# Layer two of a graph network on one core: one tile of picks in every sixteenth group becomes a gather, and the loops are four bodies long

## The reference

```python
src_feats = node_features[src]                                  # 200,000 rows of 64
messages = gelu(concatenate([src_feats, edge_features]) @ W_msg + b_msg)
agg = segment_sum(messages, tgt)
out = gelu(((1 + eps) * node_features + agg) @ W_upd + b_upd)
```

## Time and profile before

| | us |
|---|---|
| median of 3 runs | 2611.68 (2607.0 to 2617.65) |
| the profiled execution | 2620.69 |
| its span | 2618.9 |
| its loop of layer two with the last body, from the first gather to the last message sum | 1506.2 |

### The profile page before, as it was taken

The page is one execution under the profiler, slowest core; times in us unless marked ns, Lnnn a source line. Parts: engine busy times, 40 slices in busy tenths (PEclk is TensorE's granted clock), DMA queues, the critical chain, the costliest instruction groups (busy, mean ns, idle before and its releaser), DMA issues.

```text
span 2618.9 us, 70760 instructions
## 1 busy us (share of the span) xinstructions
PE 2437.3 (93%) x21749; PEld 2273.1 (87%) x21750; DVE 2012.4 (77%) x4216; ACT 1560.6 (60%) x5144; POOL 1791.4 (68%) x1879
## 2 busy tenths in 40 slices
PE   1588899999888888899999999999999999999998
PEld 1477799999888888899999999999999999999998
DVE  7888887766888886777777777777777777777774
ACT  2466666665666664566555656665656566556653
POOL 3377765677777773477777777777777777777771
PEclk9999999999999998899999999999999999999997
DMA  6111111111111110344444444445454544445451
GB/s 117 38 26 27 25 24 21 25 26 26 26 25 24 25 25 22 86 122 119 120 119 121 118 122 118 122 118 125 116 121 120 121 119 119 119 120 120 118 121 37
DMA packets 472280, 213.80 MB, mean 82 GB/s; under 512 B 264668, under 2 KB 441656, under 8 KB 472196
## 3 DMA queue, kind: packets, MB, share of 16 engines
q1 hardware_dynamic: 412548, 151.55, 22.1%
q0 software_dynamic: 59648, 61.20, 12.8%
HBM read 207.09 MB, written 5.51 MB: 81 GB/s over the span
## 4 chain that ended last, share of the span: by engine, by line
PE 58%; DVE 0%; ACT 0%; issue 0%; DVEq 0%
PE ps L930 43%; PE ps L1135 7%; PE ps L1000 4%; PE ps L1124 3%; PE ps L1082 1%; PE ps L1029 0%; DVE rows L1473 0%; DVE parts L1231 0%; DVE sel L1469 0%; DVE room L1675 0%; ACT h_sb L860 0%; DVE h_sb L1706 0%; DVE h_sb L1711 0%; ACT h_sb L878 0%; DVE tick L1510 0%
## 5 line engine op out<-in xcount | busy, mean ns | idle before, releaser
L639 POOL DMA_INDIRECT rows<-p_table,idx x1176 | 1109.8, 944 | 390.0 <-issue 342.8
L930 PE MATMUL ps<-parts,pick_all 128*128 128x448 f32 x5488 | 1162.0, 369 | 2.6 <-DVE parts L1231 2.6
L930 PEld LDWEIGHTS ps<-parts,pick_all 128*128 128x128 f32 x5488 | 1019.4, 189 | 77.7 <-issue 2.9
L639 POOL DMA_INDIRECT rows<-h_table,idx x688 | 665.3, 967 | 324.3 <-issue 200.9
L940 PE MATMUL ps<-hot_c,hot_p 128*128 128x150 f32 (+4 forms) x2336 | 435.0, 313 | 64.9 <-issue 37.1
L1469 DVE TENSOR_TENSOR sel<-ps,mask 128x896 f32<-128x896 f32 x196 | 214.0, 1092 | 307.0 <-PE ps L930 298.3
L940 PEld LDWEIGHTS ps<-hot_c,hot_p 128*128 128x128 f32 x2336 | 371.7, 192 | 85.7 <-issue 63.8
L731 ACT COPY adj<-ps 128x500 f32<-128x500 f32 (+4 forms) x880 | 349.9, 448 | 149.5 <-PE ps L940 136.9
L1452 DVE TENSOR_SCALAR pick_all<-src_all,node_f 128x1792 fp32r<-128x1792 int16 x196 | 406.5, 2074 | 27.4 <-issue 24.7
L1406 DVE TENSOR_SCALAR hot_p<-iota_p,scal 128x128 f32<-128x128 f32 (+2 forms) x880 | 301.1, 342 | 76.5 <-PE ps L940 56.0
L1473 DVE TENSOR_REDUCE rows<-sel 128x128 f32<-128x896 f32 x196 | 342.7, 1749 | 6.7
(11 more groups left out here) (182 smaller groups left out, 2345.0 us busy)
## 6 DMA issues: line engine op xcount, KB each, us to landing
src_all<-keys SPq DMA_DIRECT2D x196, 448.0 KB
ea<-in_edge_attr_dram SPq DMA_DIRECT2D x196, 256.0 KB
rows<-p_table,idx POOLq DMA_INDIRECT x1176
rows<-h_table,idx POOLq DMA_INDIRECT x688
x_sb<-in_x_dram SPq DMA_DIRECT2D x6, 224.0 KB, 4.3
h_table<-h_sb SPq DMA_DIRECT2D x6, 224.0 KB
p_table<-h_sb SPq DMA_DIRECT2D x6, 224.0 KB
out_dram<-h_sb SPq DMA_DIRECT2D x6, 224.0 KB
```

The lines of the kernel that those rows point to most:

```text
L639: nc.gpsimd.indirect_dma_start(out=rows[:, s, j, 0:D], out_offset=None, in_=table[:, :], in_offset=bass.IndirectOffsetOnAxis(ap=idx[:, s, ...
L930: last = nc.tensor.matmul(to, hot[:, k, t * P:(t + 1) * P], parts[:, part, k, :, :].rearrange("p a d -> p (a d)"), start=(k == 0 and part ...
```

## The change

In one group of sixteen (slot 3 of every fourth body) tile 6 is gathered by POOL, as tiles 0 to 5 are, and TensorE and VectorE pick tile 7 alone. That is 12 groups of 196; the last body has none. The pick matrix is still made for both tiles. The loops of POOL, TensorE and VectorE have four bodies in a pass and run 12 times; TensorE's and VectorE's announce their branch back. ScalarE's and SyncE's loops are as they were. VectorE's wait for slot 3 counts the additional gathers.

```diff
+    LOOP = 4
+        def one_pick(phase, slot):
+            return phase == LOOP - 1 and slot == SLOTS - 1
...
-                        for j in tiles:
+                        for j in range(tiles.start, tiles.stop + one_pick(phase, s)):
                             nc.gpsimd.indirect_dma_start(
...
-                    with pool.Fori(BODIES + 1, 2 * BODIES) as turn:
-                        gathers(turn, range(J0))
+                    with pool.Fori(0, (BODIES - 1) // LOOP) as i:
+                        for phase in range(LOOP):
+                            gathers(i * LOOP + (BODIES + 1 + phase), range(J0), phase)
...
-                for t in range(PICKS):
+                for t in range(one_pick(phase, q), PICKS):
...
-            with pe.Fori(0, BODIES - 1) as b:
-                second(b, False)
+            with nc.Fori(0, (BODIES - 1) // LOOP, engines=(mybir.EngineType.PE,), hint_back_edge=True) as i:
+                for phase in range(LOOP):
+                    second(i * LOOP + phase, phase, False)
...
+                own = slice(int(one_pick(phase, q)), PICKS)
+                n = PICKS - own.start
...
-                nc.vector.tensor_reduce(rows[:, q % SLOTS, J0:J, 0:D],
-                                        sel[:, :, :, :].rearrange("p t a d -> p t d a"),
+                nc.vector.tensor_reduce(rows[:, q % SLOTS, J0 + own.start:J, 0:D],
+                                        sel[:, own, :, :].rearrange("p t a d -> p t d a"),
...
+                landed = 16 * GATHERED + (b + (s + shift) // SLOTS + 1) * (16 * J0)
+                if slot == SLOTS - 1:
+                    landed = landed + (i + one_pick(phase, slot)) * 16
+                dve.wait_ge(s_gat[slot], landed)
...
-            with dve.Fori(0, BODIES - 1) as b:
-                second(b, False)
+            with nc.Fori(0, (BODIES - 1) // LOOP, engines=(mybir.EngineType.DVE,), hint_back_edge=True) as i:
+                for phase in range(LOOP):
+                    second(i * LOOP + phase, phase, False, i)
```

More of the change, by code:

```diff
@@ L184, in two_layer_gnn @@
     J0 = J - PICKS
+    LOOP = 4
+    assert (BODIES - 1) % LOOP == 0
     GATHERED = ZONES[-1].gathered(BODIES)
@@ L628, in _, with gathers @@
                 pool.wait_ge(s_tabw[layer], (UNITS + 1) * 16)
-                def gathers(turn, tiles):
+                def gathers(turn, tiles, phase=0):
                     for s in range(SLOTS):
@@ L916, in _, with picks @@
                 turn(w_raw, half, psR[half])
-            def picks(b, q):
+            def picks(b, q, phase=0):
                 hot = pick_all[:, q % 2, :].rearrange("p (k e) -> p k e", k=KA)
@@ L1142, in _, with second @@
             edge_product(0, 0, 0)
-            def second(b, last_body):
+            def second(b, phase, last_body):
                 for s in range(SLOTS):
@@ L1147, in second @@
                         edge_transpose(b, s, 1)
-                        picks(b, s + 1)
+                        picks(b, s + 1, phase)
                     last_group = last_body and s == SLOTS - 1
@@ L1165, in second @@
                             more_windows(1, b, r, lambda j, r=r: msgs[r][:, j * D:(j + 1) * D], D, 2, more)
-            with pe.Fori(0, BODIES - 1) as b:
-                second(b, False)
-            second(BODIES - 1, True)
+            with nc.Fori(0, (BODIES - 1) // LOOP, engines=(mybir.EngineType.PE,), hint_back_edge=True) as i:
+                for phase in range(LOOP):
+                    second(i * LOOP + phase, phase, False)
+            second(BODIES - 1, 0, True)
             pe.wait_ge(s_done, 2 * NG + SLOTS)
@@ L1459, in next_pick, with picked_rows @@
                 make_pick(b, q)
-            def picked_rows(b, q):
+            def picked_rows(b, q, phase=0):
                 g = b * SLOTS + q
@@ L1467, in picked_rows @@
                 dve.wait_ge(s_prow, g + 1)
[L1468 to L1471, removed]
+                own = slice(int(one_pick(phase, q)), PICKS)
+                n = PICKS - own.start
+                of = mask[:, bass.ds(g, 1), own, :].rearrange("p g t a -> p (g t) a")
+                nc.vector.tensor_tensor(sel[:, own, :, :],
+                                        ps[:, bank + own.start:bank + PICKS, 0:NA * D].rearrange(
+                                            "p t (a d) -> p t a d", d=D),
+                                        of.unsqueeze(3).to_broadcast([P, n, NA, D]), ALU.mult).then_inc(s_sel, 1)
                 dve.wait_ge(s_sel, g + 1)
-                nc.vector.tensor_reduce(rows[:, q % SLOTS, J0:J, 0:D],
-                                        sel[:, :, :, :].rearrange("p t a d -> p t d a"),
+                nc.vector.tensor_reduce(rows[:, q % SLOTS, J0 + own.start:J, 0:D],
+                                        sel[:, own, :, :].rearrange("p t a d -> p t d a"),
                                         AX.X, ALU.add).then_inc(s_prow, 1)
@@ L1664, in _, with message_sum @@
             dve.wait_ge(s_cleared, 1)
-            def message_sum(b, s, shift):
+            def message_sum(b, s, shift, phase=0, i=0):
                 slot = (s + shift) % SLOTS
@@ L1670, in message_sum @@
                 dve.wait_ge(s_em, g + 1)
-                dve.wait_ge(s_gat[slot], 16 * GATHERED
-                            + (b + (s + shift) // SLOTS + 1) * (16 * J0))
+                landed = 16 * GATHERED + (b + (s + shift) // SLOTS + 1) * (16 * J0)
+                if slot == SLOTS - 1:
+                    landed = landed + (i + one_pick(phase, slot)) * 16
+                dve.wait_ge(s_gat[slot], landed)
                 dve.wait_ge(s_prow, g + 2)
@@ L1680, in _, with second @@
             message_sum(0, 0, 0)
-            def second(b, last_body):
+            def second(b, phase, last_body, i):
                 for s in range(SLOTS):
@@ L1692, in second @@
                     if not (last_body and s == SLOTS - 1):
-                        picked_rows(b, s + 1)
-                        message_sum(b, s, 1)
+                        picked_rows(b, s + 1, phase)
+                        message_sum(b, s, 1, phase, i)
                     if s % 2:
@@ L1697, in second @@
                         sums(1, b, s, P, odd, more)
-            with dve.Fori(0, BODIES - 1) as b:
-                second(b, False)
-            second(BODIES - 1, True)
+            with nc.Fori(0, (BODIES - 1) // LOOP, engines=(mybir.EngineType.DVE,), hint_back_edge=True) as i:
+                for phase in range(LOOP):
+                    second(i * LOOP + phase, phase, False, i)
+            second(BODIES - 1, 0, True, (BODIES - 1) // LOOP)
             for u in range(UNITS + 1):
```

## The result

Before is 2613.53 us (median of 20 runs), the changed kernel 2628.85 us (20 runs). The ratio is 1.0061, 95% interval 1.0046 to 1.0076: **slower by 0.6%**, where 0.8% faster was forecast and 2608 was the top of the range. The profiled execution has a span of 2621.7 us against 2618.9.

A forecast was written before the change was run, and what follows sets the result against it. TensorE bounds, with POOL at 98% of its pace; after the change POOL's 1188 gathers plus 3 us landing bring the last sum 20.4 us sooner: 2600.3 us profiled, 2591.3 on the median's scale, range 2585 to 2608.

The forecast's parts named there:

- The bound: Layer two: TensorE busy throughout, POOL at 98% of its pace; with the added gathers POOL becomes the limit.
- The picks saved: TensorE, layer two: 14 pick products fewer in 12 groups, 2.84 us each, 34.0 us in all.
- POOL's and the landing's terms: Layer two: 1188 gathers at 1.2484 us without buffer waits, then 3 us landing (bounds 0 to 4.5) before the last sum.
- VectorE's mask and sum: VectorE in the 12 groups: 448 columns instead of 896, 1.4 us less, moving nothing in the total.
- unchanged pick matrix: VectorE still makes the pick matrix for both tiles in the 12 groups, 2.07 us: no gain.
- the zero for the branch back: New four-body loops: announced branches back cost zero, taken from TensorE's announced loops of layer one.
- Rival 3: Every TensorE branch back stalls and the clock falls: 4.55 us each, 50 in all, 2627.7 us; chance 0.10.
- VectorE's branch: VectorE's back edge costs 0.52 us ahead of its pick matrix, under its free time; stalls there would cost little.

The follow-up runs named there:

- nested: Changed kernel with TensorE's loop as an inner loop of three bodies plus the fourth body, two bodies of code, no announcement; 0.9884 of before.
- slot5: Changed kernel with the head of TensorE's layer-two loop at place 150 of its fetch block, branch back at 197; 0.9895 of before.
- two: Changed kernel with loops of two bodies on the three engines, 24 groups with the additional gather, TensorE's branch unannounced; 1.0002 of before.
- loops: Changed kernel's long loops on POOL, TensorE and VectorE without the additional gather, both tiles picked in every group; 1.0148 of before.
- silent: Changed kernel with TensorE's loop head at place 150 and TensorE's announcement taken out, VectorE's kept; 1.0118 of before.
- loops203: Changed kernel's long loops without the additional gather, TensorE's loop head at place 128, branch back at 203; 1.0017 of before.
- place60: Changed kernel with TensorE's loop head at place 13, branch back at place 60 of its fetch block; 1.0066 of before.
- place10: Changed kernel with TensorE's loop head at place 219, branch back at place 10 of its fetch block; 1.0099 of before.
- slot240: Changed kernel with TensorE's loop head at place 129 of its fetch block, branch back at 176 by the later count; 0.9913 of before.
- six: Changed kernel with passes of six bodies, one additional gather in each, TensorE's loop with an inner loop and no announcement; 0.9970 of before.
- nested2: The same kernel as nested, measured on a second occasion; 0.9923 of before.

## Why the prediction was wrong

- **The bound, right.** TensorE with POOL at 98% of its pace behind it. nested, slot5 and two show POOL's crossing with TensorE: 1486.1 us where the forecast's sum gives 1485.8, and 1500.0 for 1501.
- **The picks saved, near right**: 34.0 us. The busy time of nested in the layer is 1481.19 us against 1506.20, where 1506.2 - 34.0 = 1472.2 was expected, and that of slot5 is 1479.33. The 7 to 9 us more that are recorded as busy aren't explained by any run. loops against the changed kernel shows 30.7 of the 34.0.
- **POOL's and the landing's terms, right in size**, but without effect in the changed kernel, where the stalls let POOL's lead grow to 17 to 24 us. VectorE's mask and sum got 1.3 us shorter, forecast were 1.4; its unchanged pick matrix, put at no effect, cost TensorE the 2.8 us shown above. (One body has 450 busy records of TensorE in the earlier trace rows, not 451; nothing hangs on it.)
- **The step that failed is the zero for the branch back.** I took it "from those loops" of layer one, which announce theirs and have few gaps. They could not carry it. Their code stays loaded (45 packets in the whole run), so their announcement had nothing to do. No row of before showed an announced branch back in a loop that doesn't stay loaded. The rule of the Trainium skill, "Runtime: NRT & Kernel Launch", section "Instruction fetch mechanics", by which a taken branch out of the loaded window stalls until its block is fetched, spoke against the zero. What the runs showed in its place is 30.2 us of idle at the eleven branches, 2.7 us each, and up to 15.4 us by the clock behind seven of them. What I should have priced from both sides was how long before the branch the fetch can begin: by the packets it is 2.9 us and more in the runs that don't stall, and nothing in those with the announcement that do.
- **Rival 3 is what happened**, with a chance of 0.10. It priced a branch at 2.85 us of idle and 1.7 by the clock, 50 us in all, and 2627.7 us. Measured: 2628.85; by the trace 2.7 us of idle each, and a clock that fell behind seven of the eleven, at two of them for longer than the forecast had it. The mechanism and the idle time were right. That the totals lie so close (52.3 against 50 us) is in part luck: 2.8 us of it are the waits for the pick matrix, and 3 us of the surplus have no known cause. The rival's chance was too small, and the range ended at 2608 because of it.
- **That rule of the Trainium skill holds here for TensorE** where the branch isn't announced or is announced too late: silent and loops take 1.2 and 1.5% more. The runs add one case: announced in time, the branch costs next to nothing (loops203).
- **VectorE's branch, right in size.** VectorE's timeline after shows at most 0.9 us of idle time ahead of its pick matrix, against 0.52 before, and far from the 3.98 us of the earlier trace rows. The second instruction queue moves 109 packets with VectorE's loop of four bodies and 40 with one of two (two), so VectorE's code probably doesn't stay loaded either. Whether its announcement or something else keeps its branch free wasn't tried: no run takes the announcement away or moves its loop.

## What to carry to other kernels

Before you unroll a loop, count its loaded instructions per engine against its buffer, and look at how many instruction packets the page shows: fewer than the branches back means that the loop stays loaded, and that is worth keeping. If a longer loop is wanted on TensorE, announce its branch back and see that the branch lies late in its 256-instruction block. Count the time that passes there, not the places: in place60, 60 places of mostly skipped code before the branch gave the fetch nothing. And before you move work off the bounding engine, compute the other engine's pace from start to start and not from its busy share: POOL at 76% busy had 2% to give.

## What I had not expected

- Where a branch lies in its block is worth 2% of the whole time: place10 1.0099 against slot5 0.9895, the same instructions.
- The time after the last message sum is one of two: 34.2 to 36.8 us with the clock granted at 0.55 to 0.59 (before, slot240, nested, six, two, loops203), or 22.4 to 22.5 us at 0.91 to 0.98 (the changed kernel, slot5, nested2, place10, place60, silent, loops). nested and nested2 are one kernel, so it isn't the code. It moves the total by 12 us, as much as most of the effects here. The layer's start moves too, from 1072.07 us (six) to 1079.57 us (two) in the profiled executions. Together they are why the profiled span of after is only 2.8 us above before's while its layer is 18.3 us longer: the first gather came 3.6 us sooner, and what follows the last sum was 11.9 us shorter. What decides either wasn't tried and stays open. So the traces are best compared by the layer alone, and ratios within 0.5% of each other tell little.
- An announced branch back that doesn't stall still costs TensorE something: a pass of four bodies takes 122.99 to 123.15 us in loops203 instead of 4 x 30.69 = 122.76, 0.3 us more.
